# The prologue of an attention and mixture-of-experts kernel: the third projection, the k rows of batch 0 and GpSimd's constants change their places

## The reference, cut to what matters

```python
def attention(x, w_q, b_q, w_k, b_k, w_v, b_v, w_o, b_o):     # 16 batches, 256 tokens, 128 features, 16 heads of 8
    q, k, v = proj(w_q, b_q), proj(w_k, b_k), proj(w_v, b_v)
    scores = jnp.einsum('bhtd,bhsd->bhts', q, k) / jnp.sqrt(jnp.float32(dk))
    attn = jax.nn.softmax(scores, axis=-1)
    out = jnp.einsum('bhts,bhsd->bhtd', attn, v)
    out = out.transpose(0, 2, 1, 3).reshape(B, T, D)
    return jnp.einsum('btd,ed->bte', out, w_o) + b_o

x = x + layernorm(attention(layernorm(x), ...))
x = x + layernorm(ffn(layernorm(x), ...))      # router, 32 experts, top 6, and a shared expert
```

## Time and profile before

| | |
|---|---|
| Median of 3 runs | 540.28 us (539.05 to 540.39) |
| Profiled execution: its own time | 542.95 us |
| Profiled execution: its span | 540.9 us |
| PE busy (matmuls) | 484.6 us, 90% of the span |
| DVE busy | 398.8 us, 74% |
| ACT busy | 359.0 us, 66% |
| GpSimd busy | 170.8 us, 32% |
| Chain that ended last, by engine | PE 70%, DVE 7%, ACT 7%, SP's queue 5%, issue 5%, GpSimd 3%, DMA 2% |

### The profile page before, as it was taken

One profiled execution on the slowest core, in us unless ns is written; L12 is line 12 of the kernel. 1 busy time (PEld: TensorE's weight loads), 2 busy tenths in 40 slices (PEclk: granted clock), 3 DMA queues, 4 the chain that ended last, 5 costly groups with the idle time before them and its releaser, 6 DMA issues.

```text
span 540.9 us, 10853 instructions
## 1 busy us (share of the span) xinstructions
PE 484.6 (90%) x3376; PEld 270.5 (50%) x3376; DVE 398.8 (74%) x1072; ACT 359.0 (66%) x708; POOL 170.8 (32%) x500
## 2 busy tenths in 40 slices
PE   2457997989999999998899999999999999999993
PEld 1212443444444444444345665666656665666661
DVE  4678786879999989898725859587776859485453
ACT  2424786758888988888685566757756666755442
POOL 5054231323544435320002223515152533302020
PEclk9999999989999999999699999999999999999998
DMA  6334356333333333331014343535263544535321
GB/s 186 108 118 144 97 173 195 122 117 116 106 110 98 114 109 115 115 114 38 3 60 141 117 162 118 193 103 196 87 179 115 180 157 138 196 100 197 138 78 39
DMA packets 52456, 67.47 MB, mean 125 GB/s; under 512 B 5168, under 2 KB 36784, under 8 KB 52144
## 3 DMA queue, kind: packets, MB, share of 16 engines
q1 hardware_dynamic: 52400, 66.78, 39.2%
HBM read 51.17 MB, written 15.20 MB: 123 GB/s over the span
## 4 chain that ended last, share of the span: by engine, by line
PE 70%; DVE 7%; ACT 7%; SPq 5%; issue 5%; POOL 3%; DMA 2%; ACTq 0%; POOLq 0%; DVEq 0%
PE pY L1278 12%; PE pS L1278 12%; PE pO L1199 8%; PE pS L1264 6%; PE pS L1266 6%; PE pS L1265 6%; PE pS L1143 6%; PE pS L1149 3%; DVE mneg L859 3%; ACT probs L643 2%; SPq L387 2%; SPq L375 2%; PE pX L1128 2%; DMA k_scratch<-k_parts 2%; PE pX L1131 1%
## 5 line engine op out<-in xcount | busy, mean ns | idle before, releaser
L859 DVE TENSOR_REDUCE mneg<-pS 128x2 f32<-128x512 f32 x256 | 164.2, 686 | 31.8 <-PE pS L1143 31.0
L643 ACT ACTIVATE probs<-pS 128x512 f32<-128x512 f32 x256 | 143.9, 595 | 31.7 <-PE pS L1149 30.3
L718 ACT ACTIVATE h_ring<-r 128x512 f32<-128x512 f32 x144 | 90.4, 629 | 88.9 <-DVE r L1013 68.3
L1013 DVE SCALAR_TENSOR_TENSOR r<-pS,c_ring 128x512 f32<-128x512 f32 x128 | 87.6, 689 | 45.6 <-PE pS L1266 44.2
L1143 PE MATMUL pS<-kp,qp 48*128 48x256 bf16 x512 | 88.8, 295 | 24.9 <-DVE mneg L859 9.9
L1264 PE MATMUL pS<-qp,up_hi 128*128 128x512 f32 x144 | 103.5, 719 | 0.0
L1149 PE MATMUL pS<-qp,kp 51*128 51x256 bf16 x512 | 89.1, 287 | 0.8 <-ACT probs L643 0.5
L1199 PE MATMUL pO<-probs,vv 128*32 128x256 f32 x1024 | 76.6, 408 | 0.4 <-ACT oT_sb L594 0.4
L1278 PE MATMUL pS<-h_ring,down_sb 128*128 128x512 f32 x144 | 73.8, 594 | 0.0
L1278 PE MATMUL pY<-h_ring,down_sb 128*128 128x512 f32 x144 | 73.4, 595 | 0.0
L1143 PEld LDWEIGHTS pS<-kp,qp 48*128 48x128 bf16 x512 | 34.9, 97 | 75.3 <-DVE mneg L859 41.7
(11 more groups left out here) (178 smaller groups left out, 682.3 us busy)
## 6 DMA issues: line engine op xcount, KB each, us to landing
c_ring<-c_scratch SPq DMA_DIRECT2D x64, 512.0 KB, 3.9
qp<-q_scratch SPq DMA_DIRECT2D x64, 96.0 KB
kp<-k_scratch SPq DMA_DIRECT2D x64, 96.0 KB
q_scratch<-q_parts SPq DMA_DIRECT2D x16, 192.0 KB, 2.3
k_scratch<-k_parts SPq DMA_DIRECT2D x16, 192.0 KB, 2.4
q_scratch<-q_parts SPq DMA_DIRECT2D x16, 128.0 KB, 2.2
k_scratch<-k_parts SPq DMA_DIRECT2D x16, 128.0 KB, 2.2
out_x<-ot SPq DMA_DIRECT2D x7, 256.0 KB, 4.5
```

Of the source, the lines that this page charges most:

```text
L643: nc.scalar.activation(probs[j][:, hh], pS2[n % S2_RING][:, :, :], ACT.Exp, scale=SCALE).then_inc(exp_done, 1)
L718: nc.scalar.activation(h_sb[n % HRING], r_sb[n % URING][:, :], ACT.Square).then_inc(sq_done, 1)
L859: nc.vector.tensor_reduce(mneg[u % 2][:, :, hh, k], pS1[n % S1_RING][:, :].rearrange("p (a s) -> p a s", a=TH), AX.X, ALU.max, negate=True ...
L1013: nc.vector.scalar_tensor_tensor(out=r_sb[n % URING][:, :], in0=pU[n % URING], scalar=0.0, in1=c_ring[group % CRING][:, at], op0=ALU.max, ...
```

## The change

Five edits, all in the prologue.

- GpSimd sets vv's constants and kp's ones behind `chain_x(0)`, vv first; the small constants stay ahead.
- ACT issues the three writes of batch 0's k parts itself, behind norm_x(1) and ahead of keep_xnT(1), after a wait for part3 of batch 0. SP writes the q parts only.
- ACT issues the two loads of unit 0's k rows itself, behind part1(1) and ahead of part2(1), after waits for batch 0's six writes and for ones_set. SP loads the q rows only.
- PE runs project(2) behind the last pair of unit 0 instead of ahead of unit 0.
- DVE runs rest(2) behind the maxima of unit 0 instead of ahead of them.

write_parts and load_unit are cut into functions that take the queue (`write_q`, `write_k`, `load_rows`); for all other batches and units SP issues the same DMAs, and in load_unit both of q go ahead of both of k.

```diff
+        def write_slots(queue, b, parts, which, scratch):
...
+                queue.dma_start(dst, src).then_inc(scratch_done[b % 2], 16)
...
+        def load_rows(queue, u, ring, scratch):
+            b, half = divmod(u, 2)
+            for hh in range(2):
+                queue.dma_start(ring[u % RING][HALF * hh:HALF * hh + QK_ROWS],
+                                scratch[b, :, 2 * half + hh].rearrange("s d j t -> s d (j t)")
+                                ).then_inc(packed[u % RING], 16)
...
             def write_parts(b):
 
                 sp.wait_ge(part3_done, b + 1)
...
+                write_q(sp, b)
+                if b >= 1:
+                    write_k(sp, b)
...
+                load_rows(sp, u, qp, q_scratch)
+                if u >= 1:
+                    load_rows(sp, u, kp, k_scratch)
...
         @block.gpsimd
...
             nc.gpsimd.memset(tiny[:, 0:1], 0.0).then_inc(tiny_set, 1)
-            for i in range(RING):
-                ins = nc.gpsimd.memset(kp[i][:, :, :].rearrange("p a b -> p (a b)").bitcast(F32), ONE_TWICE)
-            ins.then_inc(ones_set, 1)
...
-            for i in range(2):
-                nc.gpsimd.memset(vv[i][:, :, :, DK + 1:VC], 0.0)
-                ins = nc.gpsimd.memset(vv[i][:, :, :, DK:DK + 1], 1.0)
-            ins.then_inc(preset, 1)
...
             chain_x(0, TH, FIRST)
+            for i in range(2):
+                nc.gpsimd.memset(vv[i][:, :, :, DK + 1:VC], 0.0)
+                ins = nc.gpsimd.memset(vv[i][:, :, :, DK:DK + 1], 1.0)
+            ins.then_inc(preset, 1)
+            for i in range(RING):
+                ins = nc.gpsimd.memset(kp[i][:, :, :].rearrange("p a b -> p (a b)").bitcast(F32), ONE_TWICE)
+            ins.then_inc(ones_set, 1)
...
                 norm_x(b)
+                if b == 1:
+                    act.wait_ge(part3_done, 1)
+                    write_k(nc.scalar, 0)
                 keep_xnT(b)
                 part1(b)
+                if b == 1:
+                    act.wait_ge(scratch_done[0], N_PARTS)
+                    act.wait_ge(ones_set, 1)
+                    load_rows(nc.scalar, 0, kp, k_scratch)
                 if b + 1 < AHEAD:
                     part2(b)
...
-            rest(2)
             for u in range(LEAD):
                 for k in range(UB):
                     for hh in range(2):
                         row_max(u, k, hh)
-                    if u == 1 and k == UB - 1:
-                        rest(AHEAD - 1)
+                    if u < 2 and k == UB - 1:
+                        rest(AHEAD - 2 + u)
...
-            for b in range(AHEAD - 1):
+            for b in range(AHEAD - 2):
                 project(b)
...
                     scores_by_query(u, k)
+                    if u == 0 and k == UB - 1:
+                        project(AHEAD - 2)
```

More of the change, by code:

```diff
@@ L306, in x1_bank, with write_q, write_k @@
             return pX[:, :] if i < 2 else pF[(i - 1) % 2]
+        def write_slots(queue, b, parts, which, scratch):
+            s = 0
+            while s < SLOTS:
+                n = 1
+                step = which[s + 1] - which[s] if s + 1 < SLOTS else 0
+                while s + n < SLOTS and step in (0, 1) and which[s + n] - which[s + n - 1] == step:
+                    n += 1
+                dst = scratch[b, s:s + n].rearrange("s u d j t -> (u d j) s t")
+                src = (parts[:, which[s]:which[s] + n, :] if n > 1 and step
+                       else parts[:, which[s]:which[s] + 1, :].to_broadcast((P, n, T)))
+                queue.dma_start(dst, src).then_inc(scratch_done[b % 2], 16)
+                s += n
+        def write_q(queue, b):
+            write_slots(queue, b, q_parts[b % 2], Q_PARTS, q_scratch)
+        def write_k(queue, b):
+            write_slots(queue, b, k_parts[b % 2], K_PARTS, k_scratch)
+        def load_rows(queue, u, ring, scratch):
[4 more added lines that the diff above has]
+                                ).then_inc(packed[u % RING], 16)
         def part3(eng, wait, b):
@@ L363, in write_parts @@
                 sp.wait_ge(part3_done, b + 1)
[L364 to L376, removed]
+                write_q(sp, b)
+                if b >= 1:
+                    write_k(sp, b)
             def load_unit(u):
-                b, half = divmod(u, 2)
+                b = u // 2
                 sp.wait_ge(scratch_done[b % 2], N_PARTS * (b // 2 + 1))
```

## The result

The changed kernel takes 544.32 us (median of 10 runs, 541.32 to 546.11) beside 540.45 us for the kernel before in the same session (10 runs, 539.05 to 542.81). The ratio is 1.0058, 95% interval 1.0037 to 1.0080, so +3.1 us (2.0 to 4.3). Measured again later, beside other runs of before, it came to 1.0071 (1.0047 to 1.0095). The forecast was +0.99 us and a range up to 543.1 us; the median lies 1.2 us above that range.

A forecast was written before the change was run, and what follows sets the result against it. A chain of waits, DVE's row maxima alternating with score matmuls, sets the loop's start; PE bounds from 50.31 us. Terms -0.95 + 0.82 - 2.31 + 3.43 = +0.99 us, from median 540.28 to 541.3 us; range 539.6 to 543.1.

The forecast's parts named there:

- The constants: DVE's layer-norm chain for batch 0: without GpSimd's memsets beside it, all that follows comes 0.95 us earlier.
- ACT's three writes: ACT ahead of its copy of xnT(1): waiting for part 3 and issuing k writes (1.58 us) costs project(1) 0.82 us.
- The moved projection: Between units 0 and 1: project(2) and rest(2) make 5.52 us instead of 2.09 to unit 1's first maximum, +3.43 us.
- GpSimd's moved memsets: GpSimd behind its norm chain: preset near 13.4 and ones_set near 16.2, ahead of the first load at 17.6, cost nothing.
- Issued at 19.6 the rows arrive near 23.1: Unit 0's k rows: 3.42 us from last load issue to PE's start, hidden up to 24.07, so maxima start at 24.70, -2.44.
- With both queues the parts have landed by about 17.7: Batch 0's q and k writes, before unit 0's loads: landed before ACT hands over part 1 of batch 1 at 18.69.
- I take 0: ACT between parts 1 and 2 of batch 1: two k loads issue while it computes, delay 0; if held, some 0.7 us.
- rival A: ACT's queue at batch 1's turn is dearer: held loads add 0.7 us, writes another 1.2, up to 543.2; chance 0.18.
- Rival B: Unit 0's k rows come late: each us beyond 24.07 delays by one; at 26.05 +3.0 in all, 543.2; chance 0.12.
- Rival C: TensorE's fast level around the loop's start: rise stays at 58.6, +0.66 (chance 0.10), or comes before the loop, -1.8 (0.07).
- Rival D: The moved projection's gap doesn't reach the loop, as something other than the maxima sets its start: only -2.44, 537.8; chance 0.05.
- The sign that the prediction had named for itself: Wrong if unit 1's maxima start before 32.9, or if the loop's start and the span move by different amounts.

The follow-up runs named there:

- the hidden write: Kernel before with constants behind GpSimd's norm chain and ACT's k writes behind keep_xnT(1), all loads on SP, projection unmoved: 539.81 beside 541.58 us, ratio 0.9963; again 0.9960.

## Why the prediction was wrong

**Right.** These steps were measured within 0.1 us of the prediction:
- The constants: L354 takes 0.17 us, and all behind DVE's chain comes 0.93 earlier (xn to part 3; 0.95 worked out).
- ACT's three writes take 1.57 us (1.58) and the copy starts at 16.17 (16.14).
- The moved projection: unit 1 stands 9.17 behind the first maximum instead of 5.77, +3.40 (+3.43), in the change and in the kernel with this part alone. DVE doesn't catch up.
- GpSimd's moved memsets cost nothing: they end at 16.15, ahead of all loads, and DVE's part 3 beside them takes 0.42 us as before.
- From unit 1 to unit 2's last pair nothing grows: +2.14 and +2.13.

**The step that failed: "The last k load was issued at 22.65 and let PE start at 26.07, 3.42 later ... Issued at 19.6 the rows arrive near 23.1".** The last k load was issued at 20.49 (19.13, and 1.36 from one load's start to the next), and the scores began 4.75 later, at 25.24. That is 2.1 us behind 23.1. The prediction had 0.97 of slack there (24.07 was its limit), so 1.17 reach the first maximum: 25.88 in place of 24.70, and from there +2.14 instead of +0.99 at unit 1. The 2.1 have three parts.

- *Some 0.4 from the writes.* "With both queues the parts have landed by about 17.7" took the distance from last issue to landing on one queue (2.1 us) and put it behind an issue halved in time. The loads resumed at 19.13, where 18.7 was counted on. Six writes from two queues fill the DMA engines (share 1.15, 340 GB/s), and the last k write takes 3.5 us to land beside 2.0 before and 2.4 with the constants moved and SP alone.
- *Some 0.4 from ACT's first load*, which took 1.32 us of issue instead of 0.94. The second took 0.71, as on SP.
- *1.3 from the landing of the rows*, 4.75 instead of 3.42. Here the engines are not full: from 20.00 to 25.24 the DMA share is 0.37, with 120 GB/s. Without ACT's queue it is 0.28 and 80 GB/s up to the first scores. By these rates some 630 KB were moved ahead of the scores instead of some 480 (an estimate), as SP puts unit 1's q rows ahead of its k rows beside ACT's loads. That this is why the k rows take longer is not tested.

The prediction cited the Trainium skill (DMA: Bandwidth & Descriptors, "Issuing engines are not separate DMA queues") and said that a strict reading changes the landing alone. By it, the trace agrees: an issue 1.5 us shorter brought the landing of the writes forward by 0.46 us (0.2 to 0.6 over all traces). The landings, of the writes and of the rows, are what the sum had mis-sized.

**Also wrong, but hidden: "Two loads of 0.94 + 0.70 us fit between 18.7 and 20.4 ... I take 0".** The half that was doubted, whether the queue issues beside its computing engine, held: L632 runs from 19.09 and the loads from 19.13. But the loads came 0.43 late and took 2.06 us, so part 2 started at 21.24 instead of 20.47, **+0.77**. This is rival A's hold, at its price of 0.7, for another reason than rival A gave. It moved the statistics' end from 24.70 to 25.47, and the k rows, 0.64 ahead of the first maximum, would have held it at 25.88 without that. The two are not added up: the later one counts.

**Rival B was the right one,** given 0.12. It said that each us of the rows beyond 24.07 is one of delay, and 25.24 gives 1.17 of the 1.18 measured. The second execution of the changed kernel bears it out (timelines of ScalarE, TensorE and VectorE):

```profile
19.00 1.32 ACTq L331 DMA_DIRECT2D kp<-k_scratch  x1
...
20.36 0.71 ACTq L331 DMA_DIRECT2D kp<-k_scratch  x1
```
```profile
24.68 0.61 PE L1163 MATMUL pS<-kp,qp 48*128 48x256 bf16 x4 [6.04 <-DMA kp<-k_scratch]
```
```profile
22.54 2.79 DVE L1063 BATCH_NORM_STATS2 stats<-xbig 128x6 f32<-128x128 f32 x14
25.32 2.68 DVE L880 TENSOR_REDUCE mneg<-pS 128x2 f32<-128x512 f32 x4
```

The rows come 0.56 earlier, and the first maximum moves by the same 0.56, to 25.32, where the statistics end as well. So between the two executions the mark at the loop (+2.13 and +1.57) follows the landing.

**Rival C** was right in kind and had the wrong place. A score matmul of the changed kernel takes 0.42 us at 60.86 and 0.28 at 62.23 (58.30 and 59.62 before): the rise follows the loop here. Behind the loop's start the rise moves the shift by up to 1.2 us in one execution, and dips of the granted clock from 90 us on by up to 2.5, which the prediction had not priced at all. The Trainium skill (TensorE: Matmul & The Clock Gate, Part 1) says that the moment varies from run to run; the traces agree, with 0.85 us between two executions of the hidden write at the split behind the rise, where their loops had started 0.02 apart. **Rival D** is excluded: each gap ahead of the loop reached its start. The sign that the prediction had named for itself, loop and span moving by different amounts, came too (+2.13 and +1.6 in the trace).

In numbers: 1.15 of the missing 2.1 us (3.1 - 0.99) are the late k rows; about 1.0 lies behind the loop's start and is open.

## What to carry to other kernels

A chain through several engines (here PE, ACT, PE, ACT, DVE) costs its whole latency if it is put between two pieces of work of the engine that sets the pace, however little work it holds; in pieces behind several of them it cost 0.9 us at the loop instead of 2.1. A second queue saved at most issue time here, so ask first whether issue or landing is what is waited for, and don't carry a landing time from one queue over to two; let a compute engine issue DMAs where it idles anyway, and not wait in its own order for a transfer to land. When two delays meet at one point, find out which ends last before adding them.

## What the runs showed of the hardware that was not expected

- ScalarE computes while its queue issues: the copy of xnT(1) at 15.45 and three DMA issues at 15.46 lie beside each other. Nothing behind the issues began before they ended: with two loads ahead of it part 2 starts at 21.24, without them at 20.47.
- The first row load that ScalarE issues takes 1.32 us of its queue and the second 0.71, in both executions of the changed kernel. On SP the first load of units 0 and 1 takes 0.94 and the later ones 0.70 to 0.74; with ScalarE's beside them the first takes 0.94 too.
- From the issue of unit 0's last k load to the first scores it takes 3.42 us before, 3.96 with only the constants moved, 4.05 with only the projection moved, and 4.3, 4.75 and 5.5 with loads on both queues (the changed kernel twice, and with the write behind the copy).
- An idle VectorE instruction of 0.19 us ahead of the loop moves its start by itself, 1.93 us for 10 of them, and these lengthen the kernel by 0.4 us (-0.7 to 1.5): a ratio of one pair of kernels is not the measure of a shift of 2 us here, the marks are.
